# Column sums by folded additions and accumulating products, with the mean taken out by products

## The reference

```
gap, gmp = mean, max over h and w
channel_weight = sigmoid(gn(w_cc @ [gap, gmp] + b_cc))
x_h, x_w = mean over w, mean over h             # 128 values per channel each
hw = w_s1 @ [x_h, x_w] + b_s1
pos_h = sigmoid(w_ph @ hw[:, :128] + b_ph);  pos_w = sigmoid(w_pw @ hw[:, 128:] + b_pw)
sx = conv3x3(gx * pos_h * pos_w) + b_s3
spatial_weight = sigmoid(gn(sx))
out = x + gx * channel_weight * spatial_weight
```

## Time and profile before

| | before |
|---|---|
| median of three runs | 4385.31 us |
| profiled execution | 4387.67 us |
| its span, first to last instruction | 4385.9 us |
| busy: PE, VectorE, ScalarE, POOL | 92%, 94%, 83%, 22% |
| mean granted TensorE clock | 0.983 |
| DMA share | 72% |
| idle VectorE before L552, waiting for loads of x | 91.8 us |

### The profile page before, as it was taken

The page is one execution under the profiler, slowest core; times in us unless marked ns, Lnnn a source line. Parts: engine busy times, 40 slices in busy tenths (PEclk is TensorE's granted clock), DMA queues, the critical chain, the costliest instruction groups (busy, mean ns, idle before and its releaser), DMA issues.

```text
span 4385.9 us, 59406 instructions
## 1 busy us (share of the span) xinstructions
PE 4041.8 (92%) x11016; PEld 1880.5 (43%) x11016; DVE 4111.8 (94%) x2975; ACT 3649.1 (83%) x7938; POOL 960.8 (22%) x2058
## 2 busy tenths in 40 slices
PE   5999999999999999999999999999999999999997
PEld 2444444444444444444444444444444444444443
DVE  7999999999999999999999999999999999999995
ACT  4888888888888888888888888888888888888886
POOL 1222222222222222222222222222222222222221
PEclk9999999999999999999999999999999999999999
DMA  7777777777777777767777777777777777777775
GB/s 124 158 172 167 168 170 166 172 166 171 167 167 171 170 169 170 169 167 173 169 170 170 167 173 169 171 168 170 167 174 168 169 169 166 175 169 170 169 171 124
DMA packets 1147900, 731.79 MB, mean 167 GB/s; under 512 B 74144, under 2 KB 1122976, under 8 KB 1147552
## 3 DMA queue, kind: packets, MB, share of 16 engines
q1 hardware_dynamic: 1147552, 728.87, 71.4%
HBM read 268.64 MB, written 268.44 MB: 122 GB/s over the span
## 4 chain that ended last, share of the span: by engine, by line
DVE 34%; issue 27%; ACT 16%; SPq 7%; PE 7%; DMA 5%; POOL 3%; DVEq 1%; ACTq 0%; POOLq 0%
DVE sums L558 9%; ACT gated L447 9%; DVE mx L615 7%; SPq L224 7%; PE conv_ps L645 6%; DMA xt<-in_x 5%; DVE sums L552 5%; DVE sp_buf L522 4%; DVE gated L566 4%; DVE sp_buf L525 4%; ACT sp_buf L354 2%; POOL rstd L277 2%; DVE gated L601 1%; ACT bias L395 1%; POOL kfac L336 1%
## 5 line engine op out<-in xcount | busy, mean ns | idle before, releaser
L645 PE MATMUL conv_ps<-gated,W_conv 128*128 128x512 f32 x6144 | 2921.0, 610 | 15.5 <-DVE gated L566 15.5
L645 PEld LDWEIGHTS conv_ps<-gated,W_conv 128*128 128x128 f32 x6144 | 1117.9, 192 | 1082.8 <-issue 1059.8
L447 ACT ACTIVATE gated<-gate_w,gate_hr 128x128 f32<-128x128 f32 x3584 | 1073.7, 389 | 153.3 <-DVE gate_hr L593 153.2
L645 PE MATMUL conv_ps<-halo,W_halo 96*128 96x512 f32 x2048 | 1040.1, 610 | 0.0
L558 DVE TENSOR_REDUCE sums<-xt 128x128 f32<-128x2048 f32 x256 | 932.5, 3683 | 0.0
L354 ACT ACTIVATE sp_buf<-conv_ps,weights 128x1024 f32<-128x1024 f32 x512 | 561.8, 1097 | 155.0 <-issue 104.5
L552 DVE TENSOR_REDUCE sums<-xt 128x16 f32<-128x2048 f32 x256 | 584.4, 2283 | 92.0 <-DMA xt<-in_x 91.8
L522 DVE SCALAR_TENSOR_TENSOR sp_buf<-xt,negm,sp_buf 128x2048 f32<-128x2048 f32 x256 | 600.6, 2346 | 36.0 <-ACT sp_buf L400 36.0
L525 DVE SCALAR_TENSOR_TENSOR sp_buf<-sp_buf,kfac,xt 128x2048 f32<-128x2048 f32 x256 | 602.1, 2352 | 9.0
L566 DVE SCALAR_TENSOR_TENSOR gated<-xt,negm,gated 128x2048 f32<-128x2048 f32 x256 | 590.7, 2349 | 3.9 <-ACT gated L447 3.9
L615 DVE TENSOR_REDUCE mx<-xt 128x2 f32<-128x4096 f32 x128 | 564.3, 4409 | 0.0
(11 more groups left out here) (80 smaller groups left out, 2229.0 us busy)
## 6 DMA issues: line engine op xcount, KB each, us to landing
xt<-in_x SPq DMA_DIRECT2D x2048, 128.0 KB, 3.0
out<-sp_buf SPq DMA_DIRECT2D x2048, 128.0 KB, 2.4
halo<-gated SPq DMA_DIRECT2D x512, 365.2 KB, 5.6
weights<-in_by_channel SPq DMA_DIRECT2D x1, 116.5 KB, 2.5
S_chan<-in_same_channel SPq DMA_DIRECT2D x1, 64.0 KB, 1.8
whalo_in<-in_wconv SPq DMA_DIRECT2D x2, 3.0 KB, 1.8
masks<-in_row_masks SPq DMA_DIRECT2D x1, 12.0 KB, 1.9
hmask<-in_halo_mask SPq DMA_DIRECT2D x1, 3.0 KB, 1.8
```

What stands on the lines that cost most here:

```text
L447: ins = nc.scalar.activation(gated[:, da, j, i, 1:1 + W], gate_w[:, da, j], ACT.Copy, scale=gate_hr[:, da, j, i:i + 1])
L645: return nc.tensor.matmul(ps, lhsT, rhs, start=start, stop=stop)
```

## The change

The kernel after no longer reduces columns in one instruction. VectorE adds rows 0 to 7 of a strip to rows 8 to 15 (fold8), then the halves of that (fold4), and leaves four rows. PE adds the four: the position product for the columns becomes four products with the same matrix that accumulate in PSUM. sums_n is gone: the division by the count is in the matrices W_rows and W_cols, and the mean is taken out by one more accumulating product each (W_rows_m, W_cols_m, undivided), whose moving operand is negm repeated over the columns. The semaphore sn_done is replaced by fold8_done and fold4_done, and `positions` waits for sums_done, fold4_done and negm_done. Row sums wait for pos_mm where they waited for sn_done. fold8 is one buffer for all blocks, fold4 has two units of two blocks.

```diff
-        sums = sb("sums", [P, 2, 2, NB + W])
-        sums_n = sb("sums_n", [P, 2, 2, NB + W])
+        sums = sb("sums", [P, 2, 2, NB])
+        fold8 = sb("fold8", [P, 8, W])
+        fold4 = sb("fold4", [P, 2, 2, 4, W])
+        W_rows_m = sb("W_rows_m", [P, P])
+        W_cols_m = sb("W_cols_m", [P, P])
...
-            link(nc.vector.tensor_copy(W_rows[:, :], pos_ps[:, 0:P]))
-            link(nc.vector.tensor_copy(W_cols[:, :], pos_ps[:, P:2 * P]))
+            link(nc.vector.tensor_copy(W_rows_m[:, :], pos_ps[:, 0:P]))
+            link(nc.vector.tensor_copy(W_cols_m[:, :], pos_ps[:, P:2 * P]))
+            link(nc.vector.tensor_scalar(W_rows[:, :], pos_ps[:, 0:P], 1.0 / W, None, ALU.mult))
+            link(nc.vector.tensor_scalar(W_cols[:, :], pos_ps[:, P:2 * P], 1.0 / NB, None, ALU.mult))
...
-                if real(a):
-
-                    dve.wait_ge(negm_done, a + 1)
-                    if later(a, 2):
-                        dve.wait_ge(pos_mm, a - 1)
-                    for j in range(2):
-                        nc.vector.tensor_scalar(sums_n[:, da, j, 0:NB], sums[:, da, j, 0:NB], 1.0 / W,
-                                                negm[:, sa, j:j + 1], ALU.mult, ALU.add)
-                        ins = nc.vector.tensor_scalar(sums_n[:, da, j, NB:], sums[:, da, j, NB:], 1.0 / NB,
-                                                      negm[:, sa, j:j + 1], ALU.mult, ALU.add)
-                    ins.then_inc(sn_done, 1)
...
-                            dve.wait_ge(sn_done, c - 1)
+                            dve.wait_ge(pos_mm, c - 1)
...
-                        nc.vector.tensor_reduce(sums[:, dc, j, NB:], xt[:, sc, j].rearrange("p b w -> p w b"), AX_X,
-                                                ALU.add).then_inc(sums_done, 1)
+                        n = 2 * c + j
+                        if later(n, 1):
+                            dve.wait_ge(fold4_done, n)
+                        nc.vector.tensor_tensor(fold8[:], xt[:, sc, j, 0:8], xt[:, sc, j, 8:16],
+                                                ALU.add).then_inc(fold8_done, 1)
+                        dve.wait_ge(fold8_done, n + 1)
+                        if later(c, 2):
+                            dve.wait_ge(pos_mm, c - 1)
+                        nc.vector.tensor_tensor(fold4[:, dc, j], fold8[:, 0:4], fold8[:, 4:8],
+                                                ALU.add).then_inc(fold4_done, 1)
...
-                        pe.wait_ge(sn_done, a + 1)
+                        pe.wait_ge(sums_done, 2 * a + 2)
+                        pe.wait_ge(fold4_done, 2 * a + 2)
+                        pe.wait_ge(negm_done, a + 1)
                         if later(a, 1):
                             pe.wait_ge(gates_done, 4 * a)
-                        mm(pos[:, :, 0:NB], W_rows[:, :], sums_n[:, da, :, 0:NB])
-                        mm(pos[:, :, NB:NB + W], W_cols[:, :], sums_n[:, da, :, NB:]).then_inc(pos_mm, 1)
+                        shift = negm[:, sa].unsqueeze(2)
+                        mm(pos[:, :, 0:NB], W_rows[:, :], sums[:, da], stop=False)
+                        mm(pos[:, :, 0:NB], W_rows_m[:, :], shift.to_broadcast([P, 2, NB]), start=False)
+                        for i in range(4):
+                            mm(pos[:, :, NB:NB + W], W_cols[:, :], fold4[:, da, :, i], start=i == 0, stop=False)
+                        mm(pos[:, :, NB:NB + W], W_cols_m[:, :], shift.to_broadcast([P, 2, W]),
+                           start=False).then_inc(pos_mm, 1)
```

More of the change, by code:

```diff
@@ L131, in conv_attention @@
         rstd_done = sem("rstd_done")
-        sn_done = sem("sn_done")
+        fold8_done = sem("fold8_done")
+        fold4_done = sem("fold4_done")
         pos_mm = sem("pos_mm")
@@ L582, in body @@
                 if real(c):
-                    dve.wait_ge(sums_done, 4 * c + 2)
+                    dve.wait_ge(sums_done, 2 * c + 2)
                     if later(c, 2):
@@ L638, in _ @@
                              stop=True).then_inc(w_pe, 1)
-            pe.wait_ge(w_dve, 27)
+            pe.wait_ge(w_dve, 29)
             pe.wait_ge(w_pool, 6)
```

## The result

The kernel after takes **4406.74 us** (median of five runs, 4405.56 to 4407.85) against 4384.67 of the kernel before (five runs beside it, 4383.63 to 4389.32): a ratio of 1.0049, 95% interval 1.0034 to 1.0063. It is 0.5% slower, on the side forecast, and 62 us under the 4469 forecast.

A forecast was written before the change was run, and what follows sets the result against it. VectorE's ring with the loads was taken to bound the kernel before. Turns of 138.0 against 135.0 gave +87, start-up -3: +84 on the profiled 4387.7, which is 2.4 above the median, so 4469 us; own range 4425 to 4505.

The forecast's parts named there:

- The ordinary unit stays at 33.3: Units away from the loop branch would still take 33.3 us, now set by a path ending in POOL's pow.
- The ring of VectorE and loads: VectorE's work plus its 8.6 us wait for loads of x, said to set 33.3 us a unit before the change.
- The added operations: Per unit, additions of 3.94 us on VectorE, hidden beside PE, and products of 1.95 us on PE.
- rival D: Additions outlast PE's cover or products are slower: +0.33 to +1.3 us a unit, 4510 to 4635 us; chance 0.12.
- Rival A: POOL's pow meets no two-input VectorE instruction: unit 32.4 us, total 4365 us; chance 0.12.
- POOL behind VectorE: POOL's pow waits until VectorE's running two-input instruction ends: next unit starts at 33.30 us, unblocked 32.4.
- No slack at the turn: At the loop branch, every four units, ScalarE's stop is no longer half made good by a 31.11 us unit.
- Rival C: ScalarE's stop at the branch is made good as before: turn 135.0 us, total 4382, no change; chance 0.10.
- The turn's price: Each loop branch costs 4.8 us beyond four ordinary units: 3.6, 0.7, 0.3 and 0.2.
- the 3.6 is paid whole: ScalarE's stop at each loop branch stays 3.6 us and adds fully to the time of the turn.
- The other terms: Per branch, PE's low clock 0.7 us, dips reaching the added products 0.3, dips behind the squares 0.2.
- +42 and +20: Upper ends in us of the forecast's range: added products at up to 2.28 us, turns at up to 5.5 us.

The follow-up runs named there:

- pow_wait: The kernel after, with VectorE held ahead of the second pass of finish(b,1) until POOL's pow is done: 4313.23 us, ratio 0.9832.
- late_halo: The kernel after, with SP held ahead of the halo copies until ScalarE has done its square: 4535.01 us, ratio 1.0334.
- small_halo: The kernel before, with halo copies of 64 elements in place of 1948, the rest left out: 4299.2 us in a single run.
- pe_alone: The kernel before with five added products issued on PE over the old operands, VectorE unchanged: 4548.76 us, ratio 1.0376.

## Why the prediction was right in its path and wrong in its size

- **The ordinary unit stays at 33.3: right**, and for the reason given. 33.31 measured. The ring of VectorE and loads is gone (wait for x 9.0 us for 91.8), the path over squares, positions, channel product, maxima, modulation, finish and pow has taken its place, and pow_wait shows its last link by removing it. The links ahead of it are read from the timeline.
- **The added operations: right.** 1.23 and 0.70 for additions put at 1.22 and 0.69; 0.43 for a 256-column product; ScalarE's second evacuation at s+17.02 for 17.1; the channel product at s+15.66 for 15.76. The additions were covered (VectorE still waits 0.57 for the product in the unit shown), so rival D stayed out. Rival A needed the request to fall outside L531; it fell 1.2 us inside.
- **POOL behind VectorE: right.** The Trainium skill, GPSIMD Engine Reference, section "8. Key points", tells of contention with VectorE instructions of two SBUF inputs. The traces agree: the same pow takes 0.55 in pow_wait and 1.58 in the unit shown after.
- **No slack at the turn: right.** The units behind a stop take 35.1 (19 of 29) or 33.4 (ten), not 31.11: nothing of the stop is made good. In the kernel before the 31.1 was not the rule I took it for: 18 of 29 units behind a stop take it, the others 33.3 to 35.0. The sum is untouched by that, since it starts from the mean turn of 135.0. Rival C had the small result for the wrong reason.
- **The turn's price: wrong, and this is the step that failed.** I wrote that "the 3.6 is paid whole". The stop is paid whole, but it is 1.31 (38.0 / 29): the largest term of the 4.8 was taken over from the kernel before as if the change could not touch it. The other terms came to 135.74 - 4 x 33.27 - 1.31 = 1.3 a turn, against 1.2 put for them (0.7, 0.3 and 0.2). Their split was off: I had put most on the convolutions at a low clock, but of the 1.8 us by which the unit shown is longer, 1.7 are the eight column products. The granted clock is 0.52 there, the level of 1.2 GHz, and they take 3.66 for 1.97. PE's timeline and the window:

```profile
2095.62 3.66 PE L648 MATMUL pos_ps<-fold,W_cols 128*128 128x256 f32 x8
...
2095.50:2099.00 3.50, 3.50 (x11) 2.85 (x11) 1.54 (x2) 2.04 (x4) 0.04 (x1) 0.52 0.46 101
```

The error of 3.6 - 1.31 = 2.3 in 29 turns is 66 us; forecast and result differ by 62.

- **The range: its upper end does not come out of its terms.** 4469 with +42 and +20 is 4531, not 4505. The miss is on the other side, below 4425, the end with turns at 3.7 us; they cost 2.7.

Why I took it for a constant: 29 stops of nearly one length looked like a price of the branch. I take it that they were equal because each met the same traffic. The change moves modulation 4.6 us sooner against s (my own sum), and the halo copies are issued as soon as it ends; I followed the loads of x through that shift, and not the copies. late_halo and small_halo show both directions: 4.0 with the copies put back, 0.56 with the copies made small. The packets show that the stop grows by the time before the packet starts. That this time is queueing behind the copies' bytes in the same DMA engines is my reading; no run separated it from other effects of traffic.

## What to carry to other kernels

When a change moves a producer, follow every DMA that it triggers to the places where another engine fetches code: here the stall at the loop's branch went with the traffic around it, not with the branch. Price the two sides of a shift of work from one engine to another apart: here VectorE's half was worth 131 us and PE's half cost 163, and doing VectorE's half alone was 3% faster than before. Where a short instruction of POOL waits for long ones of VectorE, a wait on VectorE at the right boundary can pay for itself many times.

## What the runs showed that I had not expected

- ScalarE's stop at a branch runs from 0.56 to 4.0 us with the same code, by the DMA traffic.
- A longer loop body does not only save branches: with eight iterations PE stopped 3.2 us at its turn, and in the other kernel VectorE 4.3, neither of which is seen with four.
- Five added products, 1.95 us of PE's time a unit, cost pe_alone 5.4 us a turn of four units (140.4 against 135.0) though PE has idle time left (busy 32.62 of 33.81): they stand ahead of the gates, on which the rest of the unit hangs.
